# Bounds of the scores by sign-split products added in PSUM, in a per-channel attention stage

## The reference, cut to what matters

```python
B, S, D = (4, 512, 128); H, C = (16, 64)
Q = (x @ Wq + bq).reshape(b, s, H, C) * inv_sqrt_c
K = (x @ Wk + bk).reshape(b, s, H, C)
V = (x @ Wv + bv).reshape(b, s, H, C)
scores = jnp.einsum('bshq,bshk->bshqk', Q, K)          # an outer product per token and head
mask = jnp.triu(jnp.ones((C, C), dtype=bool), 1)
w = jax.nn.softmax(jnp.where(mask, -inf, scores), axis=-1)
attn = jnp.einsum('bshqk,bshk->bshq', w, V)
x = attn.reshape(b, s, HID) @ Wo + bo
```

## Time and profile before

| | |
|---|---|
| runs | 3246.77 us median of 3 (3246.55 to 3262.4) |
| the profiled execution | 3243.49 us, its span 3239.3 us |
| granted TensorE clock, mean | 0.952 of full speed |
| channel stages of the four samples | about 1502 to 3139 us of the span |
| busy over the span | PE 83%, DVE 69%, ACT 57%, POOL 48% |

### The profile page before, as it was taken

One profiled execution on the slowest core, in us unless ns is written; L12 is line 12 of the kernel. 1 busy time (PEld: TensorE's weight loads), 2 busy tenths in 40 slices (PEclk: granted clock), 3 DMA queues, 4 the chain that ended last, 5 costly groups with the idle time before them and its releaser, 6 DMA issues. The chain is left out here.

```text
span 3239.3 us, 52421 instructions
## 1 busy us (share of the span) xinstructions
PE 2704.7 (83%) x19352; PEld 2084.0 (64%) x19352; DVE 2230.6 (69%) x4207; ACT 1852.6 (57%) x4363; POOL 1544.6 (48%) x1473
## 2 busy tenths in 40 slices
PE   1998799879987998597888888888788887898867
PEld 0565546555755575496677766777667776677766
DVE  2167516752684268434999968999699996999964
ACT  0364536553555455433787738777487774877743
POOL 0141314122422242314886728776298662986625
PEclk9999999989998999897999989999999999999989
DMA  9400000000000000182000000000000000000005
GB/s 237 129 2 1 5 10 2 1 5 10 2 1 5 11 1 1 70 302 101 4 7 1 1 4 4 7 1 1 4 4 8 1 1 5 4 8 1 1 16 171
DMA packets 75365, 93.17 MB, mean 29 GB/s; under 512 B 9324, under 2 KB 61339, under 8 KB 74984
## 3 DMA queue, kind: packets, MB, share of 16 engines
q1 hardware_dynamic: 24382, 51.53, 4.9%
q10 hardware_dynamic: 45546, 27.94, 3.6%
q0 software_dynamic: 5184, 10.29, 1.0%
HBM read 61.58 MB, written 28.62 MB: 28 GB/s over the span
## 5 line engine op out<-in xcount | busy, mean ns | idle before, releaser
L1677 POOL TENSOR_TENSOR arena<-arena 128x1536 f32<-128x1536 f32 (+9 forms) x480 | 1023.5, 2159 | 339.4 <-DVE arena L1741 246.8
L1545 PE MATMUL psum<-ident,arena 128*128 128x128 f32 (+7 forms) x7168 | 866.8, 279 | 216.4 <-ACT arena L1646 198.9
L1545 PEld LDWEIGHTS psum<-ident,arena 128*128 128x128 f32 (+7 forms) x7168 | 790.9, 137 | 322.0 <-ACT arena L1646 252.1
L1636 ACT ACTIVATE arena<-arena 128x64 f32<-128x64 f32 (+7 forms) x2048 | 707.8, 484 | 143.3 <-PE psum L1554 143.3
L1741 DVE TENSOR_TENSOR arena<-arena,psum 128x1536 f32<-128x1536 f32 (+9 forms) x480 | 494.3, 1062 | 78.8 <-ACT arena L1646 71.1
L1727 DVE TENSOR_TENSOR arena<-arena,psum 128x1536 f32<-128x1536 f32 (+9 forms) x480 | 493.5, 1061 | 23.0 <-POOL arena L1677 21.1
L894 POOL TENSOR_SCALAR arena<-arena 128x512 f32<-128x512 f32 (+3 forms) x512 | 263.9, 532 | 498.4 <-DVE arena L857 498.2
L1646 ACT ACTIVATE arena<-arena 128x1536 f32<-128x1536 f32 (+2 forms) x288 | 406.0, 1416 | 148.1 <-DVE arena L1727 148.1
L815 ACT ACTIVATE arena<-arena 128x512 f32<-128x512 f32 (+3 forms) x512 | 281.7, 552 | 183.2 <-DVE arena L850 183.2
L517 POOL TENSOR_SCALAR veps<-mv 128x1 f32<-128x1 f32 x112 | 21.5, 192 | 615.6 <-DVE mv L512 610.9
L768 PEld LDWEIGHTS psum<-ident,arena 128*128 128x128 f32 x1280 | 142.0, 144 | 169.9 <-ACT arena L826 84.7
(11 more groups left out here) (265 smaller groups left out, 3725.9 us busy)
## 6 DMA issues: line engine op xcount, KB each, us to landing
arena<-in_L_ffn_W SPq DMA_DIRECT2D x39, 768.0 KB
arena<-in_L_ffn_W SPq DMA_DIRECT2D x23, 514.0 KB
rows_d<-xrow ACTq DMA_DIRECT2D x1, 9504.0 KB, 51.9
y_d<-xrow ACTq DMA_DIRECT2D x1, 9216.0 KB
arena<-rows_d SPq DMA_DIRECT2D x62, 66.0 KB
y_d<-arena POOLq DMA_DIRECT2D x39, 64.0 KB
arena<-in_L_ffn_h_w ACTq DMA_DIRECT2D x2, 1024.0 KB
wa<-in_L_attn_W_attn ACTq DMA_DIRECT2D x1, 1536.0 KB
```

The source lines that it names most:

```text
L1545: last = nc.tensor.matmul(ps[ch.half][0:rows, to:to + P], buf[:, c:c + rows], ident[:], start=first, stop=False, is_transpose=True, skip_g ...
L1636: nc.scalar.activation(by_key[:, 0:HD - r, j], keys[:, h, 0:HD - r], ACT.Exp, bias=NB[:, j:j + 1], scale=Q3[tt % 2][:, j:j + 1]).then_inc( ...
L1677: last = nc.gpsimd.tensor_tensor(of_piece(D3[n % 5], piece), q, keys_on(K3[tt % 2], k, nk, w), ALU.mult)
```

## The change: what it does

Instead of max(q * kmax, q * kmin) the bound is computed as relu(q) * kmax - relu(-q) * kmin, which is the same number.

- ScalarE writes relu(q) and relu(-q) of each half into `QS` (columns of the weights of block 2, which are no longer needed), two more activations in `move_qk` for j = 2 and j = 3, ahead of the copy there. The copy of chunk 17 into `psM[0]` goes away.
- GpSimd multiplies them by PMX and PMN into `MQ` (`times_pool`, two multiplications of 128x512 per half), and makes NB by a subtraction (128x128). For half 1 of the next tile this stands in front of chunk 16's product, for half 0 in front of chunk 0's; at a sample's start both halves stand in front of the product of chunk 2. Before NB it waits for all own activations of the tile before.
- TensorE adds the two products in the bank, once times the identity and once times its negative (`bound_pe`, two matmuls of 128x512 per half): for half 1 of the next tile at the end of chunk 14, for half 0 at the end of chunk 0; at a sample's start after `idle_work(6, 24)`.
- VectorE's `maxima` goes away; `subtract` waits for `bound_pe` at chunk 0 and chunk 6. The scan moves from chunk 12 to chunk 11. RD, which shared a buffer with the removed QN, gets its own. The negated identity is made once, ahead of the expert stage.

```diff
+        QS = [[wa2[:, (2 * half + j) * T:(2 * half + j + 1) * T] for j in range(2)] for half in range(2)]
+        MQ = [[wa2[:, (4 + j) * T:(5 + j) * T] for j in range(2)], [wo1[:, j * T:(j + 1) * T] for j in range(2)]]
...
-        Q0_AT, MAX_0, FINISH_0, V1_AT = NC - 1, 0, 3, 3
+        FINISH_0, V1_AT = 3, 3
...
-        SCAN, MAX_1 = EARLY + 6, EARLY + 8
+
+        SCAN, TIMES_1, BOUND_1 = EARLY + 5, NC - 2, NC - 4
+        TIMES_0, BOUND_0 = 0, 0
...
+        def bound_pe(pe, tt, half):
+            pe.wait_ge(c3["mq"], 2 * tt + 2 - half)
+            if half == 0 and tt > 0:
+                pe.wait_ge(c3["d"], tt * NC)
+            nc.tensor.matmul(psM[half], ident[:], MQ[half][0], start=True, stop=False)
+            nc.tensor.matmul(psM[half], minus[:], MQ[half][1], start=False, stop=True).then_inc(c3["m"], 1)
...
             idle_work(6, 24)
+            bound_pe(pe, 0, 1)
+            bound_pe(pe, 0, 0)
             for n in range(NALL + 1):
...
                 if n == NALL:
                     break
+                if c == BOUND_0 and tt > 0:
+                    bound_pe(pe, tt, 0)
+                if c == BOUND_1 and tt + 1 < NT:
+                    bound_pe(pe, tt + 1, 1)
...
                 if tt >= 2:
                     act.wait_ge(s["prod"], (tt - 1) * NC)
+                if j >= 2:
+                    if tt > 0:
+                        act.wait_ge(s["mq"], 2 * tt + 2 - j)
+                    for to, sign in zip(QS[j - 2], (1.0, -1.0)):
+                        nc.scalar.activation(to, qk_bank(tt, j), ACT.Relu, scale=sign)
...
-                if c == Q0_AT and tt + 1 < NT:
-                    act.wait_ge(s["qk_sb"], 4 * tt + 8)
-                    act.wait_ge(s["d"], (tt + 1) * NC)
-                    nc.scalar.activation(psM[0], Q3[(tt + 1) % 2][:, 0:HB_], ACT.Copy).then_inc(s["q_ps"], 1)
...
+        def times_pool(pool, tt, half):
+            s = c3
+            pool.wait_ge(s["scan"], tt + 1)
+            pool.wait_ge(s["qk_sb"], 4 * tt + 4)
+            if tt > 0:
+                pool.wait_ge(s["m"], 2 * tt - half)
+            r = slice(half * HD // 2, (half + 1) * HD // 2)
+            for to, q, a in zip(MQ[half], QS[half], (PMX, PMN)):
+                keys = a.rearrange("p (h c) -> p c h", h=NH)[:, ::-1, :][:, r, :]
+                last = nc.gpsimd.tensor_tensor(to.rearrange("p (c h) -> p c h", h=NH),
+                                               q.rearrange("p (c h) -> p c h", h=NH), keys, ALU.mult)
+            last.then_inc(s["mq"], 1)
+            if half == 0:
+                pool.wait_ge(s["mq"], 2 * tt + 2)
+                if tt > 0:
+                    pool.wait_ge(s["own"], tt * len(own))
+                nc.gpsimd.tensor_tensor(NB, MQ[0][1][:, 0:NH * OWN], MQ[0][0][:, 0:NH * OWN], ALU.subtract).then_inc(s["neg"], 1)
...
+                if n == 2:
+                    times_pool(pool, 0, 1)
+                    times_pool(pool, 0, 0)
+                if c == TIMES_0 and tt > 0:
+                    times_pool(pool, tt, 0)
+                if c == TIMES_1 and tt + 1 < NT:
+                    times_pool(pool, tt + 1, 1)
                 if n >= 5:
                     pool.wait_ge(s["w"], n - 4)
...
             def subtract(n):
-                ch = chunks[n % NC]
+                tt, c = n // NC, n % NC
+                ch = chunks[c]
                 dve.wait_ge(s["prod"], n + 1)
+                if c == 0:
+                    dve.wait_ge(s["m"], 2 * tt + 1)
+                if c == EARLY:
+                    dve.wait_ge(s["m"], 2 * tt + 2)
...
             scan_keys(0)
-            maxima(0, 1)
-            maxima(0, 0)
             subtract(0)
             subtract(1)
```

More of the change, by code:

```diff
@@ L81, in transformer @@
         ustrict = sb("ustrict", P)
+        minus = sb("minus", P)
         ones = sb("ones", P)
@@ L224, in transformer @@
         KH = [take(NH * HD) for _ in range(2)]
-        QN = take(NH * HD // 2)
-        RD = QN
+        RD = take(NH * HD // 2)
         AT = [take(NH * HD) for _ in range(2)]
@@ L484, in transformer @@
             "d", "e", "w", "den", "num", "attn", "proj", "qk", "qk_sb", "v", "kh", "prod", "chain", "rows",
-            "own", "own_den", "own_w", "own_num", "q_ps", "neg")}
+            "own", "own_den", "own_w", "own_num", "scan", "mq", "m", "neg")}
         def x_ready(eng, stage):
@@ L1355, in experts2_dve @@
             then = in_turn(dve, s["chain"])
+            nc.vector.tensor_scalar(minus[:], ident[:], -1.0, None, ALU.mult)
             table_dve(dve, then, BLOCKS_2)
@@ L1698, in scan_keys @@
                 dve.wait_ge(s["kh"], 2 * tt + 2)
+                if tt > 0:
+                    dve.wait_ge(s["mq"], 2 * tt)
                 for dst, f, op in ((PMX, first[0], ALU.max), (PMN, first[1], ALU.min)):
                     last = nc.vector.tensor_tensor_scan(dst, f[:], KH[tt % 2], 0.0, ALU.add, op)
-                then(last)
-            def maxima(tt, half):
-                if tt == 0 or half == 1:
-                    dve.wait_ge(s["qk_sb"], 4 * tt + 4)
-                else:
-                    dve.wait_ge(s["q_ps"], tt)
-                r = slice(half * HD // 2, (half + 1) * HD // 2)
-                m, low = (a.rearrange("p (c h) -> p c h", h=NH) for a in (psM[half], QN))
-                mx, mn = (a.rearrange("p (h c) -> p c h", h=NH)[:, ::-1, :][:, r, :] for a in (PMX, PMN))
-                nc.vector.tensor_tensor(low, m, mn, ALU.mult)
-                then(nc.vector.tensor_tensor(m, m, mx, ALU.mult))
-                then(nc.vector.tensor_tensor(psM[half], psM[half], QN, ALU.max))
-                if half == 0:
-                    if tt > 0:
-                        dve.wait_ge(s["own"], tt * len(own))
-                    nc.vector.tensor_scalar(NB, psM[0][:, 0:NH * OWN], -1.0, None, ALU.mult).then_inc(s["neg"], 1)
+                last.then_inc(s["scan"], 1)
             def subtract(n):
-                ch = chunks[n % NC]
+                tt, c = n // NC, n % NC
+                ch = chunks[c]
                 dve.wait_ge(s["prod"], n + 1)
+                if c == 0:
+                    dve.wait_ge(s["m"], 2 * tt + 1)
+                if c == EARLY:
+                    dve.wait_ge(s["m"], 2 * tt + 2)
                 for piece in ch.pieces:
@@ L1772, in channel_dve @@
                 if tt > 0:
-                    if c == MAX_0:
-                        maxima(tt, 0)
                     if c == FINISH_0:
@@ L1783, in channel_dve @@
                     finish(tt, 1)
-                if tt + 1 < NT:
-                    if c == SCAN:
-                        scan_keys(tt + 1)
-                    if c == MAX_1:
-                        maxima(tt + 1, 1)
+                if c == SCAN and tt + 1 < NT:
+                    scan_keys(tt + 1)
                 if n + 2 < NALL:
```

## The result

The kernel after takes 3285.94 us, median of 4 runs (3284.76 to 3290.85); the kernel before, run beside it on the same chip, 3246.66 (3241.3 to 3262.4). The ratio is 1.0118, 95% interval 1.0093 to 1.0142: slower by 1.2%, some 39 us. The forecast was 3302 in a range of 3264 to 3338, slower with 0.85. The profiled execution took 3285.72 us, its span 3284.1.

What follows compares the result with a forecast made beforehand. It took ScalarE's 66 us plus TensorE's 27 to bound a tile. Relus 23.5 + chunk 14 3.0 - waits 3.2 + starts 31.7 + identity 0.2 is 55 us on 3243.5; median 3.3 above: 3302, range 3264 to 3338.

Steps and rivals of the forecast that it cites:

- What bounds the kernel: Whole tile: its cycle is ScalarE's 66 us plus TensorE's 27, not VectorE's busy 87.3 of 92.8 us.
- rival (a): In the tiles VectorE is the pacer after all, giving back 5.8 us per tile: 3182 us, chance 0.08.
- VectorE has slack in both stages: In a tile, VectorE's removed work, some 5.8 us per tile or 93 us over 16 tiles, lies beside other work.
- VectorE's busy time falls by 93 us: Sign over all 16 tiles: VectorE's busy share down by 93 us, its waits for ScalarE up by more.
- The starts: At each sample's start the first subtraction comes later, by 8.2, 8.2, 8.2 and 7.1 us: 31.7 us lost.
- packed products: At sample starts, GpSimd products at 1.26 instead of 1.88 us: TensorE's idle work decides, 7.9; sum 1.2 us less per start.
- Rival (c): At sample starts the delay is absorbed, while the Relus' cost is not: 3270 us, chance 0.09.
- ScalarE's Relus: In chunks 11 and 12 of 12 tiles, four more activations cost 1.96 us per tile, 23.5 us, unable to fill waits.
- Rival (d): In chunks 10 and 11, a busier TensorE keeps its clock and ScalarE's 18 us of waits go: 3284 us, chance 0.10.
- 3.0 predicted for chunk 14: TensorE's 2.00 us pair falls into the 1.74 us wait before chunk 15: 0.26 us shows, 3 us in 12 tiles.
- its waits for VectorE: In chunk 15, 5 of 12 tiles lose TensorE's wait for VectorE: 5 x 0.65 = 3.2 us given back.
- GpSimd and the scan in the tiles: In later tiles GpSimd's late products stay hidden by 4 us and the scan one chunk earlier costs nothing.

Runs made afterwards that it cites:

- e3: Kernel after with VectorE's removed products and maximum put back as idle load in chunks 14 and 0: ratio 1.0119 to the kernel before, median 3290.89 us.
- e6: Kernel after with tile 0's bounds, and tiles 1 to 3's Relus and keys' copy by head, on VectorE: ratio 1.0014 to the kernel before, 3252.37 us.
- e7: Kernel before with only the keys' copy by head moved from ScalarE to VectorE: ratio 1.0057, 3265.79 us.
- e10: e6 with the minima's scan a chunk later and GpSimd's bound products ahead of chunks 17 and 2: ratio 1.006 to the kernel before, 3276.93 us.
- e2: Kernel after, but VectorE makes tile 0's bounds at each sample's start as before: ratio 1.0046 to the kernel before, median 3263.94 us.
- e1: Kernel after with the Relus moved from ScalarE to two VectorE instructions per tile: ratio 1.0083 to the kernel before, median 3278.56 us.
- e9: Kernel before with 8 instead of 24 idle multiplications at each sample's start: ratio 1.0, 3248.76 us.
- e12: Kernel after with GpSimd's bound products ahead of chunk 0's product at a sample's start: ratio 1.0153 to the kernel before, median 3299.97 us.
- e4: Kernel after with TensorE's pair of matmuls for half 1 issued twice at every place: ratio 1.0178 to the kernel before, median 3310.04 us.
- e8: Kernel before with only the scan moved from chunk 12 to chunk 11: ratio 1.0009, 3259.25 us.

## Why the prediction was right, and where it was not

**What bounds the kernel: right.** Neither the ends of the long waits nor e3 show VectorE on the path, and rival (a) (3182) is out. The step went one sentence too far in saying that VectorE has slack in both stages: in TensorE's stage it has little. e6, e7 and e10 used it up. The sign that VectorE's busy time falls by 93 us came out at 57.0 (2230.6 to 2173.6): the moved scans took 28.5 us more than before, which the prediction had at nothing.

**The starts: right, 31.0 us against 31.7**, in part by luck. By samples the subtraction moved by 7.0, 7.5, 8.1 and 8.3 us, where 8.2, 8.2, 8.2 and 7.1 were put down. In samples 0 and 1 two errors nearly cancel. GpSimd's products took 1.54 us, not 1.88, so the first pair took 2.99 instead of 3.76. TensorE's two matmuls took 3.4 us (1532.83 to 1536.2) instead of 2.0: the rows of after show 1.69 and 1.91 us for what takes 1.02 elsewhere, after a wait of 2.55 us. In samples 2 and 3 TensorE's idle work ended 16.7 and 16.8 us behind the scan, later than GpSimd's pair, and set the start, which the prediction had only for packed products. (Its sentence that packed products would make each start 1.2 us shorter does not fit its own 8.2 and 7.9: behind the idle work only 0.3 would be left.) Rival (c) (3270) is out: ScalarE caught up with nothing there. e2 gives the price from the other side, 29.6 us.

**ScalarE's Relus: right in tiles 1 and 2, wrong in tile 0.** In the 8 tiles of the first kind ScalarE's stage grew by (266.2 + 267.3) - (259.7 + 259.8) = 14.0 us, 1.75 each where 1.96 was put down. In tile 0 it should have grown by 7.8 and fell by 0.4. There ScalarE's waits of over 0.6 us for TensorE fell from 10.8 us in the four samples (2.76 + 1.65, 2.70 + 1.71, 1.10, 0.84) to 3.4 (1.01 + 0.75, 0.84 + 0.75). This is the step that failed: the text said that the Relus could not fill such a wait, since it is for their own bank, and did not ask whether the wait would stay.

A part of it the rows do show. The two Relus of chunk 11 bring ScalarE 0.96 us later to the bank of chunk 12, and the wait for that bank is shorter by as much. Here it is in tile 2, in sample 0 before and in sample 1 after, at the same distance (53.4 us) from the tile's beginning:

```profile
1775.83 0.60 ACT L1618 ACTIVATE arena<-psum 128x512 f32<-128x512 f32 x1 [1.71 <-PE psum L1515]
```
```profile
2204.52 1.09 ACT L1644 ACTIVATE wa<-psum 128x512 f32<-128x512 f32 x2 [0.75 <-PE psum L1522]
```

Where this wait stands, it is 1.65 to 1.71 us in the kernel before and 0.75 in the kernel after, and in e1, without the Relus, it is back at 1.70 to 1.72 in tile 0 of all four samples. So two of a tile's four Relus lie in a wait wherever there is one. Rival (d) had it that the waits would go, at 18 us; of 17.7 before, 8.5 went, 7.4 of them in tile 0. With 7.4 less the forecast would have been 3294.6.

Why the larger waits went, those of 2.76 and 2.70 us, is open. Two windows of tile 0, sample 0, before: one around the wait that ends at 1576.15, and one of 4 us that just holds it. In the second fence two windows after, the first at the same distance from the tile's beginning (9 us later), the second behind it (columns of the earlier trace rows):

```profile
1568.00:1578.00 10.00, 8.01 (x44) 5.52 (x43) 10.00 (x7) 7.24 (x16) 10.00 (x4) 0.83 0.00 0
1573.00:1577.00 4.00, 4.00 (x15) 1.74 (x14) 4.00 (x3) 1.24 (x3) 4.00 (x2) 0.74 0.00 0
```
```profile
1577.00:1587.00 10.00, 9.04 (x54) 5.84 (x52) 10.00 (x6) 10.00 (x24) 10.00 (x4) 1.00 0.00 0
1592.00:1602.00 10.00, 7.70 (x39) 6.47 (x39) 10.00 (x7) 10.00 (x24) 6.62 (x5) 0.66 0.00 0
```

Before, the granted clock is 0.83 around the wait, and 0.74 in the part in which TensorE makes what ScalarE waits for and is busy 4.00 of 4.00 us. After, it is 1.00 at that place and falls, to 0.66, some 15 us later, where ScalarE is busy 10.00 of 10.00 us and waits for nobody. In these rows, then, the wait goes with the place at which the clock falls. What puts it there was not found. With less idle work at the start (e9) the waits change samples and keep their sum; with the old start (e2) a wait of 2.75 us is in all four samples; with other work at the start (e12) there is one of 3.06 in sample 0. It varies between the four samples of one kernel, and between kernels: ScalarE's stage of tile 0 took 266.5 us after and 271.2 in e3, whose samples run the same instructions up to there, and 265.3 in e4 and 271.3 in e12, whose starts differ. So of the 8 us by which tile 0 came out under the forecast, 4.7 are no more than what two such traces differ by, and the change's own part in it stays open.

**TensorE: 3.0 predicted for chunk 14, nothing measured.** An undisturbed stage is 28.4 us in both kernels. The pair took 1.96 us, and by e4 the cover was 2.25 (1.96 + 1.72 - 1.43), not the 1.74 of the one wait that I had read. TensorE's stages are 2.3 us shorter (342.6 against 344.9 over the three tiles), where 3.2 was put down for its waits for VectorE; 5 tiles of 29.1 to 29.3 had become 2.

**GpSimd and the scan in the tiles: costed at nothing, within what can be told.** e8 has the scan's move at a ratio of 0.9996 to 1.0023, so nothing or up to 7 us; its trace has 1 us of it in tile 1 of each sample. In the tiles after, the late product of chunk 0 did not reach TensorE's end: 10 of the 12 stages have the undisturbed length.

The sum in the trace: 13.6 (ScalarE) - 2.3 (TensorE) + 31.0 (starts) + 2.5 (outside the channel stage) = 44.8 us of span, where 55 was forecast. What was too high is above all tile 0's 8 us and chunk 14's 3. The median was forecast 16 us too high: 10 of them are these, 2.6 are time outside the span (4.2 us before, 1.6 after), and 3.1 come from the median, which was put 3.3 us above the profiled execution and lay 0.2 above it.

## What to carry to other kernels

An engine's busy share does not say what relieving it is worth: here VectorE, at 94% of a tile, was relieved of 5.8 us of work per tile for nothing (e3 put it back at no cost that the runs tell), while 0.5 us instructions on ScalarE at 76% were paid nearly in full in tiles 1 and 2. Cut the period at the waits that end last, price what is added to each stage, and look for places that run without the steady state's cover, such as the start of each sample, which made three quarters of this loss. At such a place look at every sample: what ends the wait in the first one need not end it in the others, and a remedy for one chain can stop at the next, as e12 did. And before spending time freed on one engine, ask how far behind the path it was: it may be the next bound.

## What the runs showed of the hardware that I had not expected

VectorE instructions with operands in SBUF alone took longer where GpSimd's products ran beside them. The scan takes 2.26 us at a sample's start, where GpSimd waits, and up to 6.6 in the kernel after (mean 2.94 before, 3.83 after); moving it by one chunk is enough (e8, 3.78). A tensor_scalar took 2.83 us instead of 0.69 (e1). The Trainium skill's "SBUF — State Buffer", section "SBUF: two separate sides", has VectorE and GpSimd share a pair of ports that one instruction locks for its whole length, when VectorE reads two operands from SBUF or runs in a two-port mode. These rows agree: the subtractions and weighings of 128x1536, one of whose operands is in PSUM, keep a mean of 1.74 to 1.75 us before and after. The range of the scan, more than its 2.26 plus one product of 3.47, is left open.

GpSimd's product with a stride of 64 elements on one operand takes 1.54 us (64 of them) against 1.26 packed (a single one), 22% more. The Trainium skill's GPSIMD Engine Reference, "Performance pitfalls for Q7 kernels", has 50% per strided element read; with one of two operands strided, the measured price is under half of that.

TensorE's clock is at its lower level in places where TensorE is busy. The granted clock was 0.74 in a window with TensorE busy 4.00 of 4.00 us (above), as it was 0.50 at 1517 to 1530 before, busy 13.00 of 13.00. At the start of sample 0 after, TensorE's pair took 3.4 us (L1546 and L1547) behind 2.55 us of waiting; in sample 2 of the same trace, and at the start of e12, right behind the idle work, the same pair took 1.9 us.
